# A two-layer kernel on Trainium2: expert rows are added to x by accumulating gathers, tiles 8 to 15 are routed in two parts, both layers share one block, and PE gets two constant matmuls per tile

## The reference

```python
x = x + _L0_xattn_ref(_layernorm(x), ctx)     # Q + tril(ctx ctx^T) @ Q, per batch
x = x + _L0_ffn_ref(_layernorm(x), w12, w3, gate_w)
x = x + _L1_xattn_ref(_layernorm(x), ctx, ctx, mask)   # softmax(x ctx^T / 16) @ ctx
x = x + _L1_ffn_ref(x, w1, b1, w2, b2)        # ternary weights, gelu, rows rounded to 8 bits

# _L0_ffn_ref: 8 experts, the best two of each row
topk_scores, topk_idx = top_k(x @ gate_w.T, 2)
topk_probs = softmax(topk_scores)
h1, h2 = halves of (x @ w12[e].T);  y += prob[e] * ((silu(h1) * h2) @ w3[e].T)
```

## Time and profile before

| | |
|---|---|
| median of three runs | 719.32 us (718.57 to 719.40) |
| profiled execution | 723.95 us, of which the span from first to last instruction is 722.0 us |
| PE / DVE / ACT / POOL busy | 78% / 73% / 51% / 51% of the span |
| mean granted clock of PE | 0.867 of full |
| indirect DMAs on POOL | 64 scatters and 64 gathers |

### The profile page before, as it was taken

One profiled execution on the slowest core, in us unless ns is written; L12 is line 12 of the kernel. 1 busy time (PEld: TensorE's weight loads), 2 busy tenths in 40 slices (PEclk: granted clock), 3 DMA queues, 4 the chain that ended last, 5 costly groups with the idle time before them and its releaser, 6 DMA issues. The chain is left out here.

```text
span 722.0 us, 17429 instructions
## 1 busy us (share of the span) xinstructions
PE 563.3 (78%) x5923; PEld 487.9 (68%) x5923; DVE 528.6 (73%) x1494; ACT 368.1 (51%) x715; POOL 365.0 (51%) x387
## 2 busy tenths in 40 slices
PE   4687955009999999999999999505668747899996
PEld 3566844008999999999999999504545523565665
DVE  6887776805866766667655655239989997999997
ACT  2499743003343443443433443204676629999994
POOL 1015275779999999998000000177773226544440
PEclk9778755559999999999999999855667979999999
DMA  5998242422222222223222222294565200011112
GB/s 196 367 356 303 62 153 79 150 90 48 61 70 65 61 69 65 62 67 68 60 68 68 60 68 67 69 340 118 171 189 158 75 1 0 16 38 38 37 39 73
DMA packets 77588, 74.80 MB, mean 104 GB/s; under 512 B 44480, under 2 KB 67904, under 8 KB 76224
## 3 DMA queue, kind: packets, MB, share of 16 engines
q1 hardware_dynamic: 71360, 56.92, 25.4%
q0 software_dynamic: 6144, 16.79, 7.3%
HBM read 40.51 MB, written 23.86 MB: 89 GB/s over the span
## 5 line engine op out<-in xcount | busy, mean ns | idle before, releaser
L906 PE MATMUL banks<-z_turned,w_of_block 128*128 128x128 f16 x3408 | 203.7, 220 | 32.9 <-DMA z_turned<-z_rows 32.9
L906 PEld LDWEIGHTS banks<-z_turned,w_of_block 128*128 128x128 f16 x3408 | 191.8, 98 | 36.1 <-issue 33.0
L994 DVE SCALAR_TENSOR_TENSOR hidden_T<-banks,blk_inv,silu_T 128x512 f32<-128x512 f32 x71 | 53.3, 751 | 117.4 <-PE banks L906 95.8
L1192 POOL DMA_INDIRECT expert_rows_in<-expert_rows,places_of_rows x64 | 64.0, 999 | 144.0 <-POOLq L1023 125.0
L403 POOL DMA_INDIRECT z_rows<-z_parts,places_in_regions x64 | 64.5, 1008 | 88.8 <-DVE places_in_regions L716 70.5
L959 ACT ACTIVATE hidden_T_high<-hidden_T 128x512 fp32r<-128x512 f32 x71 | 44.9, 632 | 109.1 <-DVE hidden_T L994 109.1
L986 DVE COPY w_of_block<-w_parts 128x4096 f16 x71 | 94.2, 1328 | 3.9 <-issue 3.9
L919 PE MATMUL banks<-w_low,hidden_T_high 128*128 x284 | 85.8, 302 | 2.8 <-DVE hidden_T_low L1000 2.7
L952 ACT ACTIVATE silu_T<-banks,blk_inv 128x512 f32<-128x512 f32 x71 | 48.8, 688 | 67.0 <-PE banks L906 66.9
L919 PE MATMUL banks<-w_high,hidden_T_high 128*128 x284 | 79.6, 280 | 0.0
L919 PE MATMUL banks<-w_high,hidden_T_low 128*128 x284 | 79.3, 279 | 0.0
(11 more groups left out here) (240 smaller groups left out, 1307.7 us busy)
## 6 DMA issues: line engine op xcount, KB each, us to landing
expert_rows<-expert_out SPq DMA_DIRECT2D x71, 128.0 KB, 1.7
w_parts<-in_w SPq DMA_DIRECT2D x7, 1024.0 KB, 7.2
x_rows<-in_x SPq DMA_DIRECT2D x8, 512.0 KB, 6.2
c_T<-in_ctx_turned SPq DMA_DIRECT2D x16, 256.0 KB, 4.1
w_low<-in_w SPq DMA_DIRECT2D x8, 512.0 KB, 8.8
c_T_in<-in_ctx_turned SPq DMA_DIRECT2D x32, 128.0 KB, 2.3
c_in<-in_ctx_rows SPq DMA_DIRECT2D x32, 128.0 KB, 3.1
out<-rows_out SPq DMA_DIRECT2D x32, 128.0 KB, 1.7
```

What stands on the lines that cost most here:

```text
L906: mm = pe.matmul(PS[:, 1 + half + 2 * u, hc * P:(hc + 1) * P], win[:, u, wp, c, at:at + P], zturn[:, j % ZB, k, :], start=(n == 0), stop=( ...
L994: v.scalar_tensor_tensor(out=g[:, :], in0=PS[:, 2 + 2 * u, :], scalar=blk_inv[:, j:j + 1], in1=s[:, :], op0=ALU.mult, op1=ALU.mult).then_i ...
L1192: pool.indirect_dma_start(rows[:, k, n, :], None, y_rows[:, :], bass.IndirectOffsetOnAxis(ap=place[:, R * i + k, n:n + 1], axis=0))\
```

## The change

- **Weights of rows.** Each row in `z_rows` carries two more numbers (its first expert's code and exp of the gap of the two scores); it is 1032 bytes long instead of 1024. SP loads them for eight blocks at a time (`load_told`), DVE makes a weight per row (`weigh`), and ACT's `keep_y` scales by it. So stored rows are weighted.
- **Gathers.** They write into `x_rows` itself with an add. The second one of a tile waits for the first to land, and the first is issued three tiles ahead (LAG = 3). `sum_rows`, `sum_rows2` and the buffer `expert_rows_in` go. DVE's moments are taken six tiles ahead (LEAD = 6), and the chain has 17 instructions.
- **Routes** are 4, 4, 4, 4, 8, 4, 4.
- **One block:** a semaphore (`w_ready` at E + 1, counted by POOL after the last `keep_y`) stands where the barrier was; POOL alone also waits for the stores.
- **PE** runs `warm` twice per tile of layer 1's attention: ones times ones, 512 columns, float16, into a bank that nobody reads.
- `b1` is split through memory, the last step's weights are loaded in halves and worked on by ACT at tiles 16 to 25, `largest_x` and the first scales move into the attention's last steps, `h_rounded` has four buffers, and h of the last four tiles is rounded in one go. POOL's scaling of weights is a tensor_tensor.

```diff
-        ROUTES = ((0, 4), (4, 8), (8, 16), (16, 24), (24, 28), (28, 32))
+        ROUTES = ((0, 4), (4, 8), (8, 12), (12, 16), (16, 24), (24, 28), (28, 32))
...
+                def exp_gaps(r):
+                    t0, t1 = ROUTES[r]
+                    act.wait_ge(picked, PICK * (r + 1))
+                    a.activation(told[:, t0:t1, 1], dl[:, t0:t1], ACT.Exp).then_inc(exped, 1)
...
+                    dve.wait_ge(exped, r + 1)
+                    for p0, p1 in pieces[r]:
+                        slots = slice(p0 % ZP, p0 % ZP + p1 - p0)
+                        v.tensor_copy(zp[:, slots, D:ZW // 2].bitcast(F32), told[:, p0:p1, :]).then_inc(told_put, 1)
...
+                def load_told(j):
+                    sp.dma_start(told_in[:, j, :], z_rows[bass.ds(rows[j], P), D:ZW // 2].bitcast(F32)).then_inc(told_got, 16)
...
                     load(j)
+                    if j % READ == 0:
+                        after(sp, weighed, WEIGH * (j // READ))
+                        for n in range(j, min(j + READ, NB)):
+                            load_told(n)
...
-                        ch.link(pool.tensor_scalar(raw[:, cols], raw[:, cols], wsc[:, e:e + 1], None, ALU.mult))
+                        ch.link(pool.tensor_tensor(raw[:, cols], raw[:, cols], wsc[:, e:e + 1].broadcast_to([P, H]), ALU.mult))
...
+                    act.wait_ge(weighed, WEIGH * (j // READ + 1))
                     act.wait_ge(yo_made, j + 1)
-                    a.activation(ye[:, u, :], PS[:, 6 + u, 0:D], ACT.Copy).then_inc(ye_made, 1)
+                    a.activation(ye[:, u, :], PS[:, 6 + u, 0:D], ACT.Copy, scale=weight[:, j:j + 1]).then_inc(ye_made, 1)
...
                 hold(0, 0)
                 hold(1, 1)
-                later[0]()
                 hidden(0, 0)
                 hold(2, 0)
                 rest_g(0, 0)
+                weigh(0)
+                later[0]()
...
+                def gather(t, n):
+                    after(pool, r_in[t % R], 32 * (t // R) + 16 * n if n else 0)
+                    pool.indirect_dma_start(X1[:, t, :], None, y_rows[:, :],
+                                            bass.IndirectOffsetOnAxis(ap=place[:, t, n:n + 1], axis=0),
+                                            compute_op=ALU.add).then_inc(r_in[t % R], 16)
+                for t in range(LAG):
+                    gather(t, 0)
...
+                for t in range(T):
+                    if t + LAG < T:
+                        gather(t + LAG, 0)
+                    gather(t, 1)
+                    if t == R:
+                        pool.memset(b3[:, :].bitcast(F32), 0.0).then_inc(magic_made, 1)
+                        pool.memset(ialT[:, :, :].bitcast(F32), 0.0).then_inc(magic_made, 1)
...
-                        if i == 0 and k >= R - 2:
-                            size_w(k - (R - 2))
-                        if i == 1 and k >= Q:
-                            (round_w, sign_w)[k % 2](k // 2 - 2)
+                        if i == 2 and k < 2:
+                            size_w(k)
+                        if (i == 2 and k >= 6) or (i == 3 and k < 2):
+                            (round_w, sign_w)[k % 2]((k + 2) // 2 % 2)
...
                         at_tile(turn, i, k, 0)
+                        warm(i)
                         at_tile(scores, i, k, 1)
                         at_tile(turn_p, i, k, 2)
+                        warm(i)
                         at_tile(product, i, k, 3)
...
+                        if s % Q != 1:
+                            at_tile(moments_x, i, k, -LEAD)
...
+                        if T - Q <= s < T + Q:
+                            largest_x(s - (T - Q))
+                        if T <= s < T + Q:
+                            advance(first_x, 2)
...
-                    if 0 <= s - 5 < T:
-                        round_h(s - 5)
+                    for t in ([s - 5] if 0 <= s - 5 < T - Q else range(T - Q, T) if s == T + 1 else ()):
+                        round_h(t)
```

More of the change, by code:

```diff
@@ L219, in layer0 @@
     moved = sbm("moved", [P, T, E], F32)
-    gone, dl, e2, r2 = (sbm(n, [P, T], F32) for n in ("gone", "gaps", "gap_exps", "gap_sums"))
+    gone = sbm("gone", [P, T], F32)
+    told_in = sbm("told_in", [P, NB, 2], F32)
+    blk_code = sbm("blk_code", [P, NB], F32)
+    hit, share = (sbm(n, [P, READ], F32) for n in ("hits", "shares"))
+    weight = sbm("row_weights", [P, NB], F32)
     shift = sbm("shift", [P, E + 1], F32)
@@ L471, in act0 @@
                         high_w12()
-                act.wait_ge(gap, 1)
-                a.activation(e2[:, :], dl[:, :], ACT.Exp).then_inc(exped, 1)
             def pe0(pe):
@@ L1342, in _, with tensor @@
                         keep_b(s // Q + 1)
-                    if 0 <= s - 6 < T and not by_dve(s - 6):
+                    if 0 <= s - 6 < T:
                         keep_ht(s - 6)
-            @block.tensor
-            def _(pe):
+            def tensor(pe):
+                pe.wait_ge(steps_done, E + 1)
                 def turn(i, k):
@@ L1393, in mid_sums @@
                     mm.then_inc(w_mid, 1)
-                group(0)
-                total(0)
-                total(1)
-                for i in range(1, NR):
+                pe.wait_ge(magic_made, 7)
+                for i in range(NR):
                     group(i)
@@ new lines, in moments_x, with norms @@
+                    v.bn_stats(stt[:, k, :], x_row(i, k)).then_inc(x2_stat, 1)
+                def norms(b):
+                    dve.wait_ge(x2_stat, Q * b + Q)
+                    after(dve, q_made, Q * b - Q)
+                    ch = Chain(dve, norms_made, LINKS * b)
+                    part = slice(b % 2 * Q, b % 2 * Q + Q)
+                    s_in = stt[:, part, :]
+                    m, vr, r, u, g = (a[:, part] for a in (mean, var, rst, tmp, gap))
+                    ch.post(v.tensor_tensor(m, s_in[:, :, 1], s_in[:, :, 4], ALU.add))
+                    ch.post(v.tensor_tensor(g, s_in[:, :, 1], s_in[:, :, 4], ALU.subtract))
+                    ch.post(v.tensor_tensor(vr, s_in[:, :, 2], s_in[:, :, 5], ALU.add))
@@ L1590, in ffn_norms @@
+                    dve.wait_ge(scales_made, 2 * n + 1)
+                    v.reciprocal(rec[:, n:n + 1], wmean[:, n:n + 1]).then_inc(scales_made, 1)
+                coming = [norms(b) for b in range(2 * NR)]
+                for k in range(Q):
+                    moments_x(0, k)
+                advance(coming[0], LINKS)
+                b1_parts()
+                for k in range(Q, LEAD):
+                    moments_x(0, k)
                 def ffn_norms(t0, t1, before):
```

445 lines of the change are left out of this document (236 added, 209 removed).

## The result

The changed kernel takes **762.82 us** (median of four, 758.47 to 764.86) against 719.36 (718.57 to 723.85): a ratio of 1.058, 95% interval 1.052 to 1.065. Slower, where 707.7 was forecast and 694 to 722 was the range. The profiled execution took 758.47 us with a span of 756.7, at the low end of its four; the profiled one of before (723.95 us, span 722.0) lay at the high end of its own. So the traces hold 34.7 of the 43 us, and I account for those.

A forecast was written before the change was run, and what follows sets the result against it. It took PE to bound the experts, DVE layer 1's attention, and POOL's scatters the end before the experts; -3.0 + 1.7 - 0.6 - 11.1 + 1.4 = -11.6 us from 719.3 gave 707.7 us, range 694 to 722.

The forecast's parts named there:

- Gathers' issue: Layer 1's attention: an accumulating gather costs POOL the same as a plain one, 1.31 us each, 2.62 us per tile.
- Rival A: Layer 1's gathers: accumulating ones are dear to issue; at half as long again the kernel takes 735 us; chance 0.13.
- Double read (+3.5): Layer 1's gathers on the DMA engines: the add reads twice, 0.13 us a tile, 3.5 us over 27 tiles.
- Last steps: End of layer 1's attention, from step 22: 14.6 us with ACT's weight work, 18.5 for nine steps, 2.7 to first gelu.
- Rival B: Layer 1's last nine steps: constants don't hold PE's clock, or landings are late; 8.1 us more, 715.8 us; chance 0.12.
- Routes (-3.0): Routing before the experts: earlier places for tiles 8 to 11 end the scatters sooner, -3.0 us, bounds 0 and -6.
- Eight bytes and weights: Experts' stage: extra loads and DVE work before block 1 expose +1.7 us, bounds 0 and +6; later weighings cost nothing.
- the sign that had been named: Experts' start: PE idle for more than 2 us after block 0 would show the +1.7 us wrong.
- POOL's cheaper scaling: Experts' stage: POOL's cheaper scaling of weights lies beside PE and changes nothing.
- One block (-0.6): Between last expert output and first gather: POOL waits for the store alone, -0.6 us, bounds 0 and -1.5.
- End of the feed-forward (+1.4): Feed-forward's end: DVE rounds four tiles in a row, delaying tile 25's finish and PE's next `down`, +1.4 us, bounds -2 and +2.
- Constants: PE in layer 1's attention: the two constant matmuls per tile get no term of their own in the gathers' shadow.

The follow-up runs named there:

- change_again: The changed kernel run once more, nothing edited, beside a kernel before of 721 us: 759.2 us, ratio 1.052.
- change_third: The changed kernel run once more in another comparison, nothing edited, beside a kernel before of 721 us: 759.6 us, ratio 1.055.
- no_constants: The changed kernel without both calls of `warm` on PE: 758.9 us, ratio 1.0535 to the kernel before.
- mixed_one_by_one: Kernel before with routes 8-12, 12-16, one block, the change's layer 1 with plain gathers, DVE adds, last four tiles rounded singly: 0.996 beside 762; 719.3 us, 0.998.

## Why the prediction was wrong, step by step

- **Gathers' issue (the step that failed).** "On POOL I price it like a plain gather, because the scatters, which go the other way, cost the same": 1.31 us per gather. Measured: 1.85 from one to the next, and 118.5 us for the 63 steps with the memsets among them. One is busy 1.544 us in the mean instead of 0.999; 58 times the difference is 31.6 us, and tile 27's moments come 113.7 us after the first gather (586.60 - 472.92) instead of 84.6: +29.1. Scatters and plain gathers are one kind of work in two directions; neither was a neighbour of an accumulating one. The mechanism was right (POOL becomes the bound); a term of the sum had no row behind it.
- **Rival A** was this, with its break-even at +0.20 us. It came at +0.54 and had a chance of 0.13. Since nothing bounded it from above, as the text itself said, that was far too low.
- **Double read (+3.5).** Not there as a pace: the gathers never wait for each other, at a mean DMA share of 0.75. The engine time behind it is there: the queue's packets hold 10.9% of 756.7 us instead of 7.3% of 722.0, some 30 us more, as much as gathers alone held before (0.36 of 82.6 us), with no more bytes counted. But gathers 1.85 us apart leave room for it; what it would do at 1.31 no run shows. The median landing rose, from 3.1 to 4.4 us.
- **Last steps (35.8 us, said to run from step 22).** 40.9 in the change (627.54 - 586.60), 5.1 too low. 3.7 of them are a step miscounted: step s takes the moments of tile s + 6, so tile 27 is taken in step 21, and step 22 masks its scores only at 590.26. From there to the mask of tile 31 (617.05) it took 26.8 us, where the working has 14.6 and six steps of 2.05, 26.9; the other 1.6 lie behind it. Rival B's clock is not it: without the constants the stretch after the last gather has 37.8 us instead of 36.0, and the kernel the same time.
- **Routes (-3.0).** Right in size: -4.6 in the trace, -3.4 alone. The first scatter of tile 8 starts at 79.92 ("near 79"), the last at 151.09 ("near 152"), and the next group is still held by its places.
- **Eight bytes and weights (+1.7, "every eighth block: nothing").** Wrong by 10 us: +5.0 at the start and +6.5 after it. At the start the mechanism was right and the sizes were not: the weights and places took 5.2 us of DVE instead of 3.3, with POOL beside it; PE also stood idle 2.12 us for block 1's load, the sign that had been named, but DVE was the later of the two. "DVE with a third of its time free" was an average; weighings of 2.5 us stand in one block. The estimate of 0.2 us for eight columns left out POOL beside it, and "POOL's cheaper scaling lies beside PE: nothing" left out DVE. After the first output the two share the loss, as above.
- **One block (-0.6).** -0.3, within what was said. The 0.2 us for the semaphore stand in no row; from the end of the last output to the first gather it took 2.49 us instead of 2.24.
- **End of the feed-forward (+1.4).** +3.4, and the four roundings are its cause; the bound of +2 was too narrow. The clock's fall was left out of it; PE is busy 1.4 us longer there (13.73 against 12.34), and whether that is all that was missed is not shown. The 1.6 us between first and last gelu is no part of the change: the same kernel has 105.9 in change_again and 107.6 in change_third.
- **Constants: no term.** Right, by no_constants.
- **Sum.** The gathers' stretch missed by 34.2 us (31.6 for the price, less the 3.5 that wasn't there, 1.0 for the rest up to tile 27's moments, 5.1 for the last steps), the experts by 9.8, the tail by 2.0, first to last gelu by 1.6, the block by 0.3, the routes by -1.6: 46.3, and 707.7 + 46.3 = 754.0 = 719.3 + 34.7. The other 8.8 us to the median are the place of the two profiled executions among their runs. With the price of a gather alone put right, the working would have said 739: slower, as measured. The runs close the account from the other side: of the 38.6 us between change_third and its kernel before, plain gathers take back 28.3; the experts' 11.5 and the tail's 3.4, less the routes' 3.4, are the rest within 1.2 us.

## What to carry to other kernels

An operation that no row of the trace shows is a guess however near its neighbours look: when it repeats 64 times on an engine that would become the bound, run it alone first, or give "dear" a chance that fits one's ignorance. Moving an add from DVE into POOL's gathers only pays where POOL has 0.6 us per gather to spare; here the free engine was traded for the one already next in line. And work put into a stage "with a third of its time free" is to be placed against the block that it falls into, with the length it has while POOL is at work beside it.

## What the runs showed of the hardware

- An accumulating gather of 128 rows keeps POOL busy 1.54 us, whether the rows have 512 or 1024 bytes; a plain one with rows of 1024 bytes 0.95. With 64 accumulating gathers the queue has twice the packets (12288 against 6144 in all), and they hold the DMA engines some 30 us of their time longer, with no more bytes counted.
- A DVE instruction of eight columns with two tensors in SBUF, begun while POOL works on a tensor, ends with POOL's instruction: 1.13 and 0.88 us at the second weighing, 0.17 and 0.12 after POOL has finished. And beside POOL's tensor_tensor DVE's copies take longer (1.58 us) than beside its slower tensor_scalar (1.38 and 1.41).
- The same kernel took 721 us on two chips and 762 to 764 on two others. The experts' stage is alike on both kinds (301.2 against 300.9 us); the routing and layer 1's attention are longer (first gather to first gelu in mixed_one_by_one 149.4 against 131.7 us), while a stretch paced by POOL's gathers is not (118.6 on either). Why is open.
